# Weight pieces on GpSimd behind z's normalising, small products ahead of the weighted values, in an attention and feed-forward kernel

## The chip, the cores and the metric

One core of one Trainium2 chip runs the whole program. The metric is the device time of one execution in microseconds; of the kernel before there are three timed runs (291.29, 291.32 and 292.5; median 291.32) and one profiled execution. Lower is better.

## The reference

Eight batches of 256 tokens with 128 features go through one transformer block. In short:

```python
def _L0_attn_ref(x, W_qkv, b_qkv, W_out, b_out, rel_bias):      # 16 heads of 8
    qkv = (x @ W_qkv + b_qkv).reshape(B, S, 3, NHEAD, D_K)
    q, k, v = (qkv[:, :, 0], qkv[:, :, 1], qkv[:, :, 2])
    scores = jnp.einsum('bihd,bjhd->bhij', q, k) / jnp.sqrt(jnp.float32(D_K))
    scores = scores + bias_by_distance        # rel_bias, clipped at 128
    attn = jax.nn.softmax(scores, axis=-1)
    out = jnp.einsum('bhij,bjhd->bihd', attn, v).reshape(B, S, D)
    return out @ W_out + b_out
def _L0_ffn_ref(x, ...):                      # ternary weights, hidden 512
    h = jax.nn.silu(_tlin(x, w1_w, w1_s)) * _tlin(x, w2_w, w2_s)
    h = jax.nn.gelu(_tlin(h, h1_w, h1_s), approximate=False)
    h = jax.nn.gelu(_tlin(h, h2_w, h2_s), approximate=False)
    return _tlin(h, w3_w, w3_s)
x = x + _layernorm(_L0_attn_ref(_layernorm(x), ...))
x = x + _layernorm(_L0_ffn_ref(_layernorm(x), ...))
```

Everything is float32. The kernel keeps the precision by splitting operands into a high part (rounded to fp32r) and the rest, the low part.

## The kernel before

The five engines run programs of their own that are written out in order; semaphores tie them together. Nothing reorders at run time: an instruction that waits holds all that stands behind it on its engine. So the order of the work is the order of the code, and a change of order on one engine can make another wait.

The program has four parts.

**Start.** x comes in units of 2, 2, 4, 4 and 4 tiles of 128 tokens. For each unit VectorE takes moments (`x_moments`), GpSimd raises the variance to the power -0.5 (`x_inv_std`, L517; this text calls it the root), VectorE normalises (`x_normalize`, L620), TensorE transposes (`x_T`), ScalarE copies the result out (`keep_xT`), and TensorE multiplies with the weights of q, k and v. For batch 0 the rows of q and k are made by products of their own with spread-out weights (`row_products`), of which ScalarE takes the high part (`take`) and TensorE then subtracts it (`row_lows`). Beside this GpSimd casts the table of the position bias to fp32r, one slot pair of heads at a time (`table_high`, L525).

**Attention, steps b = 0 to 7.** A step has 8 slots s, one pair of heads each. In slot s TensorE computes `scores(b, s)` (L1270), then for the next batch `max_scores(b + 1, s)` (L1236) and `max_bias(b + 1, s)` (L1244), from which VectorE takes the row maxima (L685). ScalarE or VectorE writes the bias into the tile of a coming slot (`write_bias`, L1015 and L692), ScalarE takes the exponential (`probabilities`, L1008). The three tiles `place0` to `place2` go round: the maximum products of a slot may start when the exponential of the slot before is done, since they use its tile. After every second slot the values of two slot pairs are weighted (`weighted(b, g)`, L1296, group g of 4), and ScalarE copies the group out (`keep_weighted`, L1020). Between these stand the small products of the batch before: `back` (L1307, transposes of oT), `heads_T`, `project` (L1320), `maxima_T` (L1253, the transposed maxima, which ScalarE copies in `minus_max`), `norm_T` (L1327, transposes of z). The layer norms behind the projection run on VectorE in slots 4 to 6: `attn_moments`, `residual`, `second_norm`, the last of which normalises z (L620) and sets `z_set`.

**Splitting of the weights.** Eleven pieces of the feed-forward weights are split into high and low part by GpSimd (`split_weights`, L559 to L571, four instructions each, all reading the on-chip memory), in steps 1 to 6: 1, 1, 2, 3, 3 and 1 of them. In a step they stand behind the two roots that GpSimd computes for the layer norms.

**Feed-forward.** Four chunks of 512 tokens; `gate`, `layer1`, `layer2`, `layer3` on TensorE (L1441, L1442), in an order written out in `ffn`. The last batch's attention output (`heads_T`, `project`, the two norms, `norm_T`) is threaded through it.

## Time and profile before

| | us |
|---|---|
| median of three runs | 291.32 |
| the profiled execution | 292.18 |
| its span in the trace | 290.4 |
| TensorE busy | 268.5 (92%) |
| VectorE busy | 219.3 (76%) |
| ScalarE busy | 205.9 (71%) |
| GpSimd busy | 102.4 (35%) |
| start, to 31 us: TensorE busy | 28.88 |
| steps 1 to 6, 54 to 178 us: TensorE busy | 117.45 of 124.00 |
| the same: VectorE busy | 108.94 |
| the same: ScalarE busy | 91.22 |
| feed-forward, from 194 us: TensorE busy | 86.37 of 96.40 |
| ScalarE idle ahead of oT's copies (L1020), waiting for the weighted values | 22.1, 18 times |

The profiled execution is 1.8 us longer than its span: that is what lies around the recorded work. Busy times are sums over an engine; what a change is worth is not read from them but from the waits in the stretch where it acts. A row of a timeline gives start, length, engine, line, operation, output and input, the count of merged instructions, and in brackets how long the engine stood idle before it and what ended that. PE is TensorE (PEld its loading of weights), DVE VectorE, ACT ScalarE, POOL GpSimd. TensorE's clock was granted whole through the attention part (1.00, which is the 2.4 GHz level).

### The profile page before, as it was taken

The numbers are of one execution on the slowest core, as the hardware profiler recorded it, in microseconds if no ns is written. First come the engines' busy times: TensorE is split into PE (matmuls) and PEld (weight loads), VectorE is DVE, ScalarE is ACT, GpSimd is POOL, SyncE is SP. The second block draws the span as 40 slices with busy tenths as digits, with TensorE's granted clock in tenths as the row PEclk, the third lists the DMA queues.
The fourth block names the chain that finished last, engine by engine and source line by source line (L and its number), as shares of the span: only waits on it lengthen the run. The fifth ranks groups of instructions, "written<-read, shape, count | busy, mean of one in ns | idle before, by whom it ended". The sixth has DMA issues, their size and how long they took to land.

```text
span 290.4 us, 5171 instructions
## 1 busy us (share of the span) xinstructions
PE 268.5 (92%) x1875; PEld 180.4 (62%) x1875; DVE 219.3 (76%) x442; ACT 205.9 (71%) x316; POOL 102.4 (35%) x107
## 2 busy tenths in 40 slices
PE   7999989899999999999998998899999999999980
PEld 7756645555555554565554554567887888888860
DVE  3489977889789889889889899848556843673674
ACT  2777777776786786885886876777469976896750
POOL 7616000103504305906966957018630202400111
PEclk9999999999999999999999999999999999999996
DMA  6979506232221263470320200000000000010012
GB/s 166 320 238 142 184 11 208 89 83 77 74 76 38 77 207 124 138 224 8 104 81 19 61 1 3 1 3 1 0 2 0 0 0 2 0 36 2 2 36 77
DMA packets 21356, 21.17 MB, mean 73 GB/s; under 512 B 3664, under 2 KB 18768, under 8 KB 21072
## 3 DMA queue, kind: packets, MB, share of 16 engines
q1 hardware_dynamic: 20464, 20.53, 24.8%
q8 instruction: 17, 0.28, 0.4%
q10 hardware_dynamic: 864, 0.27, 0.4%
q14 instruction: 11, 0.09, 0.1%
HBM read 14.90 MB, written 5.64 MB: 71 GB/s over the span
## 4 chain that ended last, share of the span: by engine, by line
PE 60%; DVE 22%; ACT 9%; issue 5%; DMA 1%; POOL 0%; SPq 0%; ACTq 0%; DVEq 0%
PE place L1441 10%; PE place L1442 10%; PE place L1244 8%; DVE mx L685 7%; PE pv L1296 6%; PE place L1236 4%; ACT ring L1008 4%; DVE y_and_z L620 4%; PE place L1270 4%; DVE stats L609 2%; PE place L1195 2%; DVE place L692 2%; ACT place L1015 2%; PE pv L1442 2%; PE pv L1441 2%
## 5 line engine op out<-in xcount | busy, mean ns | idle before, releaser
L685 DVE TENSOR_REDUCE mx<-place 128x4 f32<-128x1024 f32 x64 | 78.1, 1222 | 13.1 <-PE place L1244 11.8
L517 POOL TENSOR_TENSOR rstd<-mv,mhalf 128x2 f32<-128x2 f32 (+1 forms) x26 | 21.0, 809 | 153.0 <-DVE mv L617 153.0
L1008 ACT ACTIVATE ring<-place 128x1024 f32<-128x1024 f32 x64 | 65.6, 1027 | 6.3 <-PE place L1281 3.0
L1244 PE MATMUL place<-room,identr 128*128 128x512 f32 x128 | 46.9, 447 | 0.0
L1015 ACT COPY place<-raw 128x1024 f32<-128x1024 f32 x37 | 37.7, 1022 | 12.2 <-DVE mx L685 11.9
L1441 PE MATMUL place<-room,w_hi 128*128 128x512 f32 (+1 forms) x116 | 44.6, 387 | 0.7 <-DVE room L818 0.7
L1442 PE MATMUL place<-room,w_hi 128*128 128x512 f32 (+1 forms) x116 | 44.0, 382 | 0.0
L818 DVE TENSOR_TENSOR room<-ring,room 128x512 fp32r<-128x512 f32 x32 | 21.4, 690 | 18.5 <-ACT room L1096 18.5
L1296 PE MATMUL pv<-ring,vx 128*9 128x256 f32 x512 | 33.6, 380 | 0.0
L1270 PE MATMUL place<-room 33*128 33x256 f32 x256 | 31.7, 328 | 1.1 <-DVE place L692 1.0
L1236 PE MATMUL place<-room 33*128 33x256 f32 x256 | 28.3, 297 | 2.9 <-ACT ring L1008 2.7
L1270 PEld LDWEIGHTS place<-room 33*128 33x128 f32 x256 | 18.9, 184 | 15.4 <-issue 12.2
L1020 ACT COPY oT<-pv 128x256 f32<-128x256 f32 x32 | 11.8, 370 | 22.2 <-PE pv L1296 22.1
L1236 PEld LDWEIGHTS place<-room 33*128 33x128 f32 x256 | 19.8, 185 | 10.1 <-issue 6.8
L1441 PEld LDWEIGHTS place<-room,w_hi 128*128 128x128 f32 x116 | 21.8, 188 | 5.1 <-DVE room L818 0.9
L1244 PEld LDWEIGHTS place<-room,identr 128*128 128x128 f32 x128 | 19.0, 188 | 8.6
L1442 PEld LDWEIGHTS place<-room,w_hi 128*128 128x128 f32 x116 | 21.8, 188 | 4.1
L692 DVE COPY place<-raw 128x1024 f32<-128x1024 f32 x19 | 23.2, 1225 | 0.6
L1094 ACT ACTIVATE ring<-place,hs 128x512 f32<-128x512 f32 x27 | 18.5, 686 | 5.9 <-PE place L1442 5.9
L1296 PEld LDWEIGHTS pv<-ring,vx 128*9 128x9 f32 x512 | 10.9, 90 | 17.3 <-issue 9.9
L830 DVE SCALAR_TENSOR_TENSOR ring<-place,hs,raw 128x512 f32<-128x512 f32 x16 | 12.0, 750 | 12.0 <-ACT raw L1073 11.8
L1096 ACT CAST room<-ring 128x512 fp32r<-128x512 f32 x32 | 19.9, 621 | 1.0
(141 smaller groups left out, 442.9 us busy)
## 6 DMA issues: line engine op xcount, KB each, us to landing
raw<-ext SPq DMA_DIRECT2D x8, 384.0 KB, 6.9
room<-q_parts SPq DMA_DIRECT2D x48, 64.0 KB
room<-k_parts SPq DMA_DIRECT2D x48, 64.0 KB
w_lo<-h SPq DMA_DIRECT2D x2, 1024.0 KB, 5.2
q_parts<-w_hi SPq DMA_DIRECT2D x4, 256.0 KB, 3.0
k_parts<-w_hi SPq DMA_DIRECT2D x2, 512.0 KB, 3.4
xs<-x SPq DMA_DIRECT2D x3, 256.0 KB, 5.7
w_lo<-w SPq DMA_DIRECT2D x3, 256.0 KB, 2.7
```

What stands on the lines that cost most here:

```text
L517: nc.gpsimd.tensor_tensor(rstd[:, at:at + width], mv[:, at:at + width, 1], mhalf[:, 0:width], ALU.pow).then_inc(rstd_set, 1)
L685: nc.vector.tensor_reduce(mx[:, s // RPAIRS, :, :, s % RPAIRS].rearrange("p i k -> p k i"), max_tile(b * PAIRS + s)[:, :, :].rearrange("p ...
L692: nc.vector.tensor_copy(score_tile(i)[:, :, :].rearrange("p k (j n) -> p k j n", j=2), pair_windows(raw[:, :, :], i % PAIRS)).then_inc(bia ...
L818: nc.vector.tensor_tensor(lo, act_f[:, half[c], k, :], hi.bitcast(F32), ALU.subtract).then_inc((a1_lo_set, a2_lo_set)[i], 1)
L1008: nc.scalar.activation(probs[:, s % PRING, :, :, :].rearrange("p k j n -> p (k j n)"), score_tile(b * PAIRS + s)[:, :, :].rearrange("p k n ...
L1015: nc.scalar.copy(score_tile(i)[:, :, :].rearrange("p k (j n) -> p k j n", j=2), pair_windows(raw[:, :, :], i % PAIRS)).then_inc(bias_set, 1)
L1236: mm(max_tile(b * PAIRS + s)[:, half, it * S:(it + 1) * S], rows(q_rows, b, half, s)[:, it * P:(it + 1) * P], rows(k_rows, b, half, s), st ...
L1244: last = mm(max_tile(b * PAIRS + s)[:, half, :], identr[:, :], windows(table_hi[:, 2 * s + half, :], 0, P, 2, S), start=False, stop=True, ...
L1270: last = mm(tile[:, half, j * S:(j + 1) * S], rows(k_rows, b, half, s)[:, j * P:(j + 1) * P], rows(q_rows, b, half, s), start=(s in BY_PE ...
L1296: last = mm(pv[32 * r:32 * r + VC, 0:S], vx[:, b * TPB + j, 4 * g + r, :], probs[:, (2 * g + r // 2) % PRING, r % 2, j, :], start=(j == 0) ...
L1441: mm(o, w, hi, start=first, stop=False)
L1442: done = mm(o, w, lo, start=False, stop=last and exact)
```

## The change

Six edits, all of order:

- GpSimd, start: the table's casts of slots 0 and 1 come ahead of the root of x's unit 2, and those of slots 6 and 7 wait until unit 3 is normalised (`xn_set` at 4).
- GpSimd, steps 1 to 6: the pieces of weights wait until z of the step is normalised (`z_set` at b).
- VectorE, start: moments of unit 1 behind the first normalising and the spread weights; `minus_ident` ahead of the second normalising.
- TensorE, start: both `row_products` and `row_lows(0)` ahead of the transposes of unit 1.
- TensorE, steps 0 to 6, slots 0, 2, 4 and 6: the weighted values come at the slot's end, behind the small products. In step 7 they stay. ScalarE copies group 3 behind the transposed maxima in steps 1 to 6.
- Feed-forward: the last `project` stands behind three outputs of layer 1 of chunk 1 and not two, and VectorE's last `attn_moments` behind one low part of that layer.

```diff
@@ -530,11 +530,16 @@
             pool.wait_ge(row_zeros, 1)
             spread_weights(nc.gpsimd.tensor_copy, 1)
             x_inv_std(1)
+            table_high(0)
+            table_high(1)
             x_inv_std(2)
-            for s in range(PAIRS):
+            for s in range(2, 6):
                 table_high(s)
-                if s == 5:
-                    x_inv_std(3)
+            x_inv_std(3)
+
+            pool.wait_ge(xn_set, 4)
+            table_high(6)
+            table_high(7)
             for i, s in enumerate(BY_PE):
                 pool.wait_ge(table_hi_pool, s + 1)
                 nc.gpsimd.tensor_tensor(table_lo[:, 2 * i:2 * i + 2, :], raw[:, 2 * s:2 * s + 2, :],
@@ -575,6 +580,8 @@
                 if b > 0:
                     inv_std((b - 1) * 2 + NU + 1, TPB)
                     inv_std((b - 1) * 2 + NU + 2, TPB)
+
+                    pool.wait_ge(z_set, b)
                 for piece in SPLIT_AT[b]:
                     split_weights(piece)
 
@@ -658,11 +665,11 @@
             x_moments(0)
             dve.wait_ge(qk_w_in[0], 16)
             nc.vector.tensor_scalar(wq_sb[:, :], wq_sb[:, :], scale, None, ALU.mult).then_inc(bq_scaled, 1)
-            x_moments(1)
             x_normalize(0)
             dve.wait_ge(row_zeros, 1)
             dve.wait_ge(bq_scaled, 1)
             spread_weights(nc.vector.tensor_copy, 0, (0,))
+            x_moments(1)
             dve.wait_ge(brows_in, 16)
             nc.vector.tensor_scalar(brows_sb[:, 0, 0:PAIRS], brows_sb[:, 0, 0:PAIRS], scale, None,
                                     ALU.mult).then_inc(brows_scaled, 1)
@@ -670,9 +677,9 @@
             nc.vector.tensor_tensor(low_bias[:, :, :], brows_sb[:, :, 0:PAIRS],
                                     brows_sb[:, :, PAIRS:PAIRS + 1].broadcast_to((P, 2, PAIRS)),
                                     ALU.mult).then_inc(low_bias_set, 1)
-            x_normalize(1)
             dve.wait_ge(ident_loaded, 16)
             nc.vector.tensor_scalar(minus_ident[:, :], ident[:, :], -1.0, None, ALU.mult).then_inc(minus_set, 1)
+            x_normalize(1)
             dve.wait_ge(qk_w_in[2], 16)
             nc.vector.tensor_scalar(bq_sb[:, 0:1], bq_sb[:, 0:1], scale, None, ALU.mult).then_inc(bq_scaled, 1)
             nc.vector.tensor_copy(identr[:, :], ident[:, :]).then_inc(identr_set, 1)
@@ -859,8 +866,9 @@
             gate_product(2, 3)
             gate_low(2, 3)
             layer_low(0, 0)
+            layer_low(1, 0, (0,))
             attn_moments(B - 1)
-            layer_low(1, 0, (0, 1))
+            layer_low(1, 0, (1,))
             residual(B - 1)
             layer_low(1, 0, (2, 3))
             second_norm(B - 1)
@@ -1036,9 +1044,11 @@
                         write_bias(ahead)
                     probabilities(b, s)
                     if s == 0:
-                        if b > 0:
+                        if b + 1 == B:
                             keep_weighted(b - 1, GROUPS - 1)
                         minus_max(b, 1)
+                        if 0 < b < B - 1:
+                            keep_weighted(b - 1, GROUPS - 1)
                     if b == 0:
                         if s == 1:
                             keep_xT(3)
@@ -1204,10 +1214,10 @@
 
             pe.wait_ge(xT_set, 1)
             row_products(0)
+            row_products(1)
+            pe.wait_ge(minus_set, 1)
+            row_lows(0)
             x_T(1)
-            pe.wait_ge(minus_set, 1)
-            row_products(1)
-            row_lows(0)
             pe.wait_ge(xT_set, 2)
             q_and_k(1, 0)
             q_and_k(1, 1)
@@ -1326,6 +1336,13 @@
                 for it in range(TPB):
                     last = nc.tensor.transpose(misc[:, it * P:(it + 1) * P], z[:, it, :], ident[:, :])
                 last.then_inc(zT_ready, 1)
+
+            def values(b, s):
+
+                if s > 0:
+                    weighted(b, s // 2 - 1)
+                elif b > 0:
+                    weighted(b - 1, GROUPS - 1)
 
             pe.wait_ge(identr_set, 1)
             for s in range(PAIRS):
@@ -1375,17 +1392,14 @@
 
                         scores(b, s + 1)
                         score_bias(b, s + 1)
+                    if s % 2 == 0 and not more:
+                        values(b, s)
                     if s == 0:
-                        if b > 0:
-                            weighted(b - 1, GROUPS - 1)
                         if b > 1:
                             pe.wait_ge(z_lo_set, b - 1)
                         if b == 0:
                             pe.wait_ge(qk_lo_set, 4)
                         maxima_T(b, 1)
-                    else:
-                        if s % 2 == 0:
-                            weighted(b, s // 2 - 1)
                     if b > 0:
                         if s == 1:
                             pe.wait_ge(mrow_set, b * RANGES + 2)
@@ -1432,6 +1446,8 @@
                         else:
                             pe.wait_ge(mrow_set, b * RANGES + 3)
                         norm_T(b - 1)
+                    if s % 2 == 0 and more:
+                        values(b, s)
             weighted(B - 1, GROUPS - 1)
 
             def product(o, weight, x, exact, first=True, last=True):
@@ -1560,9 +1576,9 @@
                 gate(2, 3, exact)
                 heads_T(B - 1)
                 layer1(0, 3, exact)
-                whole(layer1, 1, exact, (0, 1))
+                whole(layer1, 1, exact, (0, 1, 2))
                 project(B - 1)
-                whole(layer1, 1, exact, (2, 3))
+                layer1(1, 3, exact)
                 whole(layer2, 0, exact)
                 layer2(1, 0, exact)
                 pe.wait_ge(y_read, B)
```

On TensorE, in slots 2 to 4 of a middle step, the rows before are these (pv is the weighted values, misc<-ident,oT is `back`, misc<-ident,on `heads_T`, misc<-wo_sb,onT `project`, the place rows are scores, maximum products and maximum bias):

```order
L1236 MATMUL place<-room 128x256 x4
L1244 MATMUL place<-room,identr 128x512 x2
L1296 MATMUL pv<-ring,vx 9x256 x8
L1307 MATMUL misc<-ident,oT 128x128 x4
L1270 MATMUL place<-room 128x256 x4
L1236 MATMUL place<-room 128x256 x4
L1244 MATMUL place<-room,identr 128x512 x2
L1314 MATMUL misc<-ident,on 128x128 x2
L1270 MATMUL place<-room 128x256 x4
L1236 MATMUL place<-room 128x256 x4
L1244 MATMUL place<-room,identr 128x512 x2
L1296 MATMUL pv<-ring,vx 9x256 x8
```

and in the changed kernel, ten lines further down in the file:

```order
L1246 MATMUL place<-room 128x256 x4
L1254 MATMUL place<-room,identr 128x512 x2
L1317 MATMUL misc<-ident,oT 128x128 x4
L1306 MATMUL pv<-ring,vx 9x256 x8
L1280 MATMUL place<-room 128x256 x4
L1246 MATMUL place<-room 128x256 x4
L1254 MATMUL place<-room,identr 128x512 x2
L1324 MATMUL misc<-ident,on 128x128 x2
L1280 MATMUL place<-room 128x256 x4
L1246 MATMUL place<-room 128x256 x4
L1254 MATMUL place<-room,identr 128x512 x2
L1330 MATMUL misc<-wo_sb,onT 128x128 x2
```

In slot 2 the second `back` and in slot 4 `project` now stand ahead of the eight products of the weighted values. Slot 3 is as it was.

On TensorE at the start (misc<-ident,xn are the transposes of x, place<-ring,w_lo the row products, minus_ident the low rows, wq_sb and wk_sb unit 1's q and k), before:

```order
L1169 MATMUL misc<-ident,xn 128x128 x2
L1162 MATMUL place<-blank 128x256 x3
L1195 MATMUL place<-ring,w_lo 128x256 x2
L1169 MATMUL misc<-ident,xn 128x128 x2
L1195 MATMUL place<-ring,w_lo 128x256 x2
L1202 MATMUL place<-z_parts,minus_ident 128x512
L1174 MATMUL place<-ring,wq_sb 128x256
L1174 MATMUL place<-ring,wk_sb 128x256
```

and now:

```order
L1179 MATMUL misc<-ident,xn 128x128 x2
L1172 MATMUL place<-blank 128x256 x3
L1205 MATMUL place<-ring,w_lo 128x256 x4
L1212 MATMUL place<-z_parts,minus_ident 128x512
L1179 MATMUL misc<-ident,xn 128x128 x2
L1184 MATMUL place<-ring,wq_sb 128x256
L1184 MATMUL place<-ring,wk_sb 128x256
```

The second transposes, of unit 1, moved behind the second row products and the first low rows; q and k of unit 1 follow right behind them.

On VectorE at the start (L609 and L616 are the moments, L620 and L627 the normalising), before:

```order
L660 TENSOR_SCALAR wq_sb<-wq_sb 128x128
L609 BN_STATS stats<-xs 128x6 x2
L613 BN_AGGR mv<-stats 128x2 x2
L617 TENSOR_SCALAR mv<-mv 128x2
L620 TENSOR_SCALAR xn<-xs,mv,rstd 128x128 x2
L382 COPY w_lo<-wq_sb 128x8x32
L667 TENSOR_SCALAR brows_sb<-brows_sb 128x8
L670 TENSOR_TENSOR low_bias<-brows_sb 128x16
L620 TENSOR_SCALAR xn<-xs,mv,rstd 128x128 x2
L675 TENSOR_SCALAR minus_ident<-ident 128x128
```

and now:

```order
L667 TENSOR_SCALAR wq_sb<-wq_sb 128x128
L627 TENSOR_SCALAR xn<-xs,mv,rstd 128x128 x2
L382 COPY w_lo<-wq_sb 128x8x32
L616 BN_STATS stats<-xs 128x6 x2
L620 BN_AGGR mv<-stats 128x2 x2
L624 TENSOR_SCALAR mv<-mv 128x2
L674 TENSOR_SCALAR brows_sb<-brows_sb 128x8
L677 TENSOR_TENSOR low_bias<-brows_sb 128x16
L681 TENSOR_SCALAR minus_ident<-ident 128x128
L627 TENSOR_SCALAR xn<-xs,mv,rstd 128x128 x2
```

The first normalising and the spread weights moved ahead of the second moments, which stand ahead of the bias rows; `minus_ident` moved ahead of the second normalising.

## Rows read from the trace of the kernel before

**Rows 1.** The chain of waits of step 5: start us, length us, what
```profile
138.03 0.51 PE place L1236 x4
...
145.00 0.36 ACT oT L1020
...
147.38 0.50 PE place L1236 x4
...
148.55 0.98 PE pv L1296 x16
...
149.53 0.66 PE misc L1320 x4
```

**Rows 2.** Timeline of VectorE, normalising (columns as above under the table)
```profile
23.73 3.75 DVE L620 TENSOR_SCALAR xn<-xs,mv,rstd 128x128 f32<-128x128 f32 x4
...
53.45 1.12 DVE L620 TENSOR_SCALAR xn<-xs,mv,rstd 128x128 f32<-128x128 f32 x4
...
155.78 1.74 DVE L620 TENSOR_SCALAR y_and_z<-xs,mv,rstd 128x128 f32<-128x128 f32 x2
```

**Rows 3.** Timeline of TensorE, step 5
```profile
143.53 1.05 PE L1296 MATMUL pv<-ring,vx 128*9 128x256 f32 x16
...
152.22 0.30 PEld L1236 LDWEIGHTS place<-room 33*128 33x128 f32 x4 [0.28 <-ACT ring L1008]
...
155.53 1.09 PE L1281 MATMUL place<-room,identr 128*128 128x512 f32 x4
...
157.68 0.41 PE L1327 MATMUL misc<-ident,y_and_z 128*128 128x128 f32 x2 [1.06 <-DVE y_and_z L620]
...
158.36 0.40 PE L1236 MATMUL place<-room 33*128 33x256 f32 x4
```

**Rows 4.** Timeline of ScalarE and TensorE, end of step 2
```profile
94.68 1.03 ACT L1008 ACTIVATE ring<-place 128x1024 f32<-128x1024 f32 x1 [0.34 <-PE place L1281]
...
94.99 0.44 PE L1327 MATMUL misc<-ident,y_and_z 128*128 128x128 f32 x2 [0.35 <-DVE w_hi L640]
...
95.85 0.50 PE L1236 MATMUL place<-room 33*128 33x256 f32 x4
```

**Rows 5.** Timeline of GpSimd, end of step 5's pieces and the next root
```profile
168.89 1.27 POOL L571 TENSOR_TENSOR xn<-xn,w_hi 128x512 f32<-128x512 f32 x1
...
171.93 0.73 POOL L517 TENSOR_TENSOR rstd<-mv,mhalf 128x2 f32<-128x2 f32 x1 [1.77 <-DVE mv L617]
```

**Rows 6.** Timeline of ScalarE, slots 4 and 5 of step 5
```profile
149.60 0.37 ACT L1020 COPY oT<-pv 128x256 f32<-128x256 f32 x1 [1.17 <-PE pv L1296]
...
150.19 1.02 ACT L1015 COPY place<-raw 128x1024 f32<-128x1024 f32 x1 [0.23 <-DVE mx L685]
```

**Rows 7.** Timeline of step 0, slots 3 to 6
```profile
44.42 0.74 DVE L640 SCALAR_TENSOR_TENSOR w_hi<-misc,bq_sb,w_hi 128x512 fp32r<-128x512 f32 x1
...
45.63 1.16 PE L1180 MATMUL misc<-wv_sb,xT 128*128 128x128 f32 x8
...
45.76 0.37 ACT L1020 COPY oT<-pv 128x256 f32<-128x256 f32 x1 [0.87 <-PE pv L1296]
...
48.60 0.40 PE L1236 MATMUL place<-room 33*128 33x256 f32 x4
```

**Rows 8.** Timeline of the start
```profile
5.21 1.20 POOL L382 COPY w_lo<-wk_sb 128x256 f32<-128x256 f32 x2
...
6.57 0.60 DVE L620 TENSOR_SCALAR xn<-xs,mv,rstd 128x128 f32<-128x128 f32 x2
...
10.35 0.37 ACT L940 COPY ring<-misc 128x256 f32<-128x256 f32 x1
...
10.84 0.63 PE L1174 MATMUL place<-ring,wq_sb 128*128 128x256 f32 x2
```

**Rows 9.** Timeline of TensorE, the last projection
```profile
220.12 0.71 PE L1320 MATMUL misc<-wo_sb,onT 128*128 128x128 f32 x4 [0.69 <-ACT onT L1024]
```

## The prediction

> **What bounds the kernel now.** I read the chain of waits of one middle step of the attention loop first, then the timelines of TensorE, ScalarE and VectorE through that step, and at last those of the start, the first step and the place of the last projection. Steps are called 0 to 7 (one batch each), slots are the eight head pairs of a step. All times below are in step 5, which TensorE's maximum products open at 138.03, unless said.
>
> TensorE is the busiest engine, but it runs in a ring with ScalarE: the maximum products of a slot go into the tile that the exponential of the slot before has left. The chain [rows 1] shows what this means: at 145.00 ScalarE copies the first group of weighted values out (oT), then writes a bias, then does an exponential, and only at 147.38 TensorE goes on with slot 4's maximum products. Behind these the path runs through the weighted values (0.98) and the projection (0.66), and at the step's end through z's normalising on VectorE. The reader is to see that two things of the change lie on this chain, z and the order of values and projection, and that a third lies on it too: the copy oT, which is fed by the very product that the change puts back.
>
> **GpSimd's pieces behind z's normalising.** z's two instructions take 1.74 beside GpSimd's pieces; four such instructions without company take 1.12 at 53.45, so two take 0.56, and about 1.2 us per step leave VectorE. At 23.73 four take 3.75, beside GpSimd's casts of the bias table [rows 2]. How much of that reaches TensorE? In step 5 it waits 1.06 for z, but its maximum products of the next step, at 158.36, also wait for slot 7's exponential, which waits for the score bias that ends at 155.53 plus 1.09, 156.62 [rows 3]. In step 2 that second wait is seen bare: the exponential starts at 94.68, z's transposes come late by 0.35, and the maximum products start at 95.85, 1.17 after the exponential's start [rows 4]. So in steps 2 to 4 the faster z gives nothing; in step 5 the products could start at 158.0, 0.35 earlier, and step 6 is alike. Gain 0.8 at the highest, and only if the ring is not later by then.
>
> The Trainium skill (SBUF — State Buffer, Who interferes with whom) says that VectorE's copies and tensor_scalar in their 2-port modes take the port pair that GpSimd uses, whoever comes first holding it for a whole instruction. The 3.75 against 1.12 agrees. By that rule the change also makes new collisions at the start; they are priced from rows below.
>
> The last instruction of step 5's pieces now begins at 168.89 and takes about 1.3; the next root is asked for at 171.93 [rows 5]. That is 1.8 of room, against pieces that start later by z's own time and one hand-over, about 1.2. It fits; if not, the root is late by a few tenths, and VectorE behind it has 1.2 in hand from z.
>
> **Small products ahead of the weighted values, steps 1 to 6.** TensorE's total is the same, but ScalarE runs in order, and its copy of a group waits for the weighted values. Slot 2: group 0's values start at 143.53 and the transposes behind them take about 0.6 [rows 3]. Exchanged, with 0.15 of wait for VectorE's `on` ahead, the values end at about 145.33 and the copy starts at 145.40, not at 145.00. This copy is on the chain, so slot 4's maximum products are 0.40 later. Slot 4: the values ended at 149.53 [rows 1]; with the 0.40 and the projection's 0.66 ahead they end at 150.59. The copy, which waited 1.17 for them already, starts at 150.66 and not at 149.60. The bias of slot 6 behind it, which started at 150.19 because VectorE's maximum held it [rows 6], now waits for the copy. In [rows 1] the maximum products start 2.38 behind the copy's start; from 150.66 that is 153.04, against 152.22 [rows 3]: +0.82. The hand-over at slot 6 is shorter (2.03 from the bias's start, and 0.26 for the copy ahead of it), which gives 152.95, +0.73. I take 0.75. From there TensorE has no idle time to the step's end, so steps 1 to 4 lose it whole: 3.0. In steps 5 and 6 the wait for z covers most: the score bias ends at 157.37, the exponential starts at 157.41, the maximum products at 158.58 against 158.36. That is 0.2 each, 0.4, and holds z's gain already.
>
> What comes back? The projection is earlier for VectorE, but VectorE is at its maximum of slot 4 until just before 150.19, as ScalarE's wait for it shows [rows 6], and the projection ended at 150.19 as well [rows 1]: the add of y starts there either way. Bounds of this part: nothing if all is absorbed, 0.82 for each of four steps at the top.
>
> **Step 0.** Here q's product goes ahead of group 0 and v's ahead of group 1. v must wait for k's low part, which VectorE finishes at 44.42 plus 0.74, 45.16. TensorE would be there at about 44.3 (the values began 0.98 ahead of v's 45.63, and q's lead gives 0.3 to 0.4), and idles where the values stood. v runs from 45.2 to 46.3, the values to 47.3, the copy starts at 47.4 (was 45.76), and the maximum products 2.3 to 2.4 later, at 49.75 against 48.60 [rows 7]: +1.15. At the least 0, if k's low part came a whole us earlier, which q's lead is too small for.
>
> **The start.** x's first normalising no longer stands behind the second load. Its root is there when GpSimd goes on at 5.21, so it may start at 5.3 and not at 6.57; but GpSimd copies weights until 6.41, and by the slow instructions of [rows 2] it gets through about 0.4 earlier, not 1.2. Against that the transposes of unit 1 now stand behind the low rows, which wait for ScalarE's taking. Before, ScalarE's xT copy stood right behind that taking, at 10.35, and q's product of unit 1 at 10.84 [rows 8]. Now low rows 0.4, transposes 0.4, and two hand-overs of 0.07 come in between: +0.95. Less 0.4 that is 0.55, and two casts of the table beside x's second normalising may add to it; bounds -0.4 (the collision costs nothing and the order nothing) and +1.0; I take 0.6. The later normalising at 23.73 frees VectorE 2.6 earlier, but TensorE's row products set the pace there: 0.
>
> **The feed-forward part.** The last projection waits 0.69 for onT [rows 9]; behind one more output of layer 1 it doesn't, and the engine is full behind it: -0.6 (bounds -0.7 and 0). VectorE's last moments move behind one more low part; z's transposes come only after five outputs of layer 2, which covers it.
>
> **Sum.** 0.6 + 1.15 + 3.0 + 0.4 - 0.6 = +4.5. The profiled execution took 292.18 (span 290.4 and 1.8 around it), which gives 296.7. It is 0.86 above the median of 291.32, so for the median the forecast is 295.8.
>
> **Rivals.**
> Faster: VectorE's chain is the true bound, and the ring with ScalarE has slack that the rows don't show. For it speaks that the chain of waits walks through values, projection and z. Then the waits at z go: 1.06 and as much in step 6, 0.35 and as much in two more, 3.1 in all; with start and feed-forward even, this is 288.2. Against it: ScalarE's copy is on the same chain, and in step 2 the maximum products start with the exponential whatever z does.
> No change: the values' delay is swallowed, and start, z and projection cancel: 0.6 - 0.8 - 0.6, plus something in step 0, about 291. What decides is whether slot 6's maximum products stay at 14.2 us behind the step's first (152.22 less 138.03).
> Worse: the later pieces reach the next root in steps 4 and 5, which have three each, and cost a us there on top: 298.
>
> **Chances.** Forecast 0.62, faster 0.18, no change 0.15, worse 0.05. What a measurement can tell here is about 0.5%, 1.5 us. From the cases: faster 0.19, same 0.18, slower 0.63. The slower case's own range is 293.4 to 297.6 (0.4 to 0.82 for each step, the start at -0.1 to 1.0, step 0 from 0.6). For 8 in 10 it reaches down to 289.8, which leaves out most of the faster rival and the worse one.
>
> **What would show it.** z's two instructions at 0.6 in steps 2 to 6. ScalarE's copy of group 1 waiting 1.9 or more for TensorE where it waited 1.17. TensorE's maximum products in a middle step 0.4 later at slot 4 and 0.75 at slot 6, counted from the step's first. The three steps from 95.85 to 158.36 take 62.5 now, 20.8 each; I expect 64.2. A TensorE gap of 0.9 ahead of v in step 0. q of unit 1 at 11.4. No wait at the last projection. I am wrong if those three steps take 62.5 or less, or if q of unit 1 starts before 10.84.

## The result and the profile after

The changed kernel takes 293.22 us (median of six, 292.96 to 294.12) against 291.87 for the kernel before beside it: ratio 1.0052 [1.0037, 1.0068], slower by 1.5 us. The forecast was 295.8, slower by 4.5. Ratios, and the differences in us that are worked out from them, leave out the few runs that fell in a slower state, while medians and ranges hold them, so that the two can differ by some tenths. The profiled execution took 293.34 (before 292.18), with a span of 291.4 (before 290.4).

The first place to look was the distance between the openings of the steps (the maximum products of slot 0 on TensorE; in step 7, which has none, the weighted values in their place, at 178.66 and 181.53), since a loss in the loop must stand there:

| stretch | before | after | change | forecast |
|---|---|---|---|---|
| q of unit 1 starts | 10.84 | 11.44 | +0.60 | +0.60 |
| from there to step 1's opening (54.12; 55.75) | 43.28 | 44.31 | +1.03 | +1.15 |
| step 1 | 20.65 | 20.99 | +0.34 | +0.75 |
| step 2 | 21.08 | 21.47 | +0.39 | +0.75 |
| step 3 | 21.07 | 21.46 | +0.39 | +0.75 |
| step 4 | 21.11 | 21.48 | +0.37 | +0.75 |
| step 5 | 20.33 | 20.21 | -0.12 | +0.20 |
| step 6 | 20.30 | 20.17 | -0.13 | +0.20 |
| step 7 and on to the last transposes of heads | 34.91 | 34.94 | +0.03 | 0 |
| from there to z's last transposes, in the feed-forward part | 19.83 | 18.87 | -0.96 | -0.60 |

They add up to +1.94, and VectorE's last instruction ends 1.95 later too (288.90 against 286.95). The span is only 1.0 longer, because the output's transfer behind that instruction took 2.5 us in this trace and 3.45 in that of before. So a single pair of traces is good to a microsecond at its end, and the distances between openings to some hundredths.

TensorE in step 5 of the changed kernel, start and length, with the idle time before and what ended it; this answers to [rows 1, 3]:

```profile
141.15 0.50 PE L1246 MATMUL place<-room 33*128 33x256 f32 x4 [0.55 <-ACT ring L1016]
...
146.66 0.66 PE L1317 MATMUL misc<-ident,oT 128*128 128x128 f32 x4
147.25 1.05 PE L1306 MATMUL pv<-ring,vx 128*9 128x256 f32 x16
...
150.76 0.50 PE L1246 MATMUL place<-room 33*128 33x256 f32 x4 [0.45 <-ACT ring L1016]
151.19 0.73 PE L1254 MATMUL place<-room,identr 128*128 128x512 f32 x2
151.77 0.61 PE L1330 MATMUL misc<-wo_sb,onT 128*128 128x128 f32 x4
152.30 1.05 PE L1306 MATMUL pv<-ring,vx 128*9 128x256 f32 x16
...
155.72 0.51 PE L1246 MATMUL place<-room 33*128 33x256 f32 x4 [0.39 <-ACT ring L1016]
...
159.05 1.10 PE L1291 MATMUL place<-room,identr 128*128 128x512 f32 x4
159.99 0.38 PE L1337 MATMUL misc<-ident,y_and_z 128*128 128x128 f32 x2
...
161.36 0.50 PE L1246 MATMUL place<-room 33*128 33x256 f32 x4 [0.56 <-ACT ring L1016]
```

z's transposes wait for nothing now, and the opening behind them waits 0.56 for the exponential instead. Slot 4 waits 0.45 (it was 0.22) and slot 6 waits 0.39; before, the products of slot 6 showed no wait, but the load of their weights waited 0.28 [rows 3]. ScalarE beside it, answering to [rows 6]:

```profile
148.37 0.37 ACT L1028 COPY oT<-pv 128x256 f32<-128x256 f32 x1 [0.24 <-PE pv L1306]
...
153.42 0.37 ACT L1028 COPY oT<-pv 128x256 f32<-128x256 f32 x1 [1.62 <-PE pv L1306]
153.69 1.02 ACT L1023 COPY place<-raw 128x1024 f32<-128x1024 f32 x1
154.64 1.03 ACT L1016 ACTIVATE ring<-place 128x1024 f32<-128x1024 f32 x1
```

The copy at 153.42 waits 1.62 where it waited 1.17, and bias and exponential follow it without a break. In the chain of waits (start, length, what) the path goes through just these:

```profile
152.37 1.03 PE pv L1306 x16
153.40 0.02 issue
153.42 0.03 ACT oT L1028
153.45 0.24 issue
153.69 0.16 ACT place L1023
153.85 0.79 issue
154.64 1.04 ACT ring L1016
155.68 0.04 issue
155.72 0.51 PE place L1246 x4
```

Over the whole kernel, TensorE's idle time ahead of the maximum products rises from 2.9 to 7.4 (columns: busy, mean ns | idle before, releaser). The 4.5 more is not all loss: z's waits, which are gone, were 3.1 together, and TensorE is 1.4 us less busy in all (267.1 against 268.5).

```profile
L1246 PE MATMUL place<-room 33*128 33x256 f32 x256 | 28.5, 299 | 7.4 <-ACT ring L1016 7.4
L1028 ACT COPY oT<-pv 128x256 f32<-128x256 f32 x32 | 11.9, 373 | 29.4 <-PE pv L1306 29.3
```

VectorE and GpSimd. z's two instructions in step 5, then the normalising at the start and that of unit 3, answering to [rows 2, 8]:

```profile
5.32 1.20 DVE L627 TENSOR_SCALAR xn<-xs,mv,rstd 128x128 f32<-128x128 f32 x2 [0.76 <-POOL rstd L517]
...
8.51 1.08 DVE L627 TENSOR_SCALAR xn<-xs,mv,rstd 128x128 f32<-128x128 f32 x2 [0.38 <-POOL rstd L517]
...
24.38 1.11 DVE L627 TENSOR_SCALAR xn<-xs,mv,rstd 128x128 f32<-128x128 f32 x4
...
158.96 0.60 DVE L627 TENSOR_SCALAR y_and_z<-xs,mv,rstd 128x128 f32<-128x128 f32 x2
```

1.74 has become 0.60 and 3.75 has become 1.11, while the first two, which moved beside GpSimd's work, take twice what they took. GpSimd's pieces start behind z, and the root behind step 5's pieces still finds the engine free, as those behind steps 1 to 4 do (with 1.48 us and more to spare), answering to [rows 5]:

```profile
174.90 0.72 POOL L517 TENSOR_TENSOR rstd<-mv,mhalf 128x2 f32<-128x2 f32 x1 [0.62 <-DVE mv L624]
```

Start, step 0 and the last projection, answering to [rows 7 to 9]:

```profile
11.44 0.70 PE L1184 MATMUL place<-ring,wq_sb 128*128 128x256 f32 x2 [0.46 <-ACT ring L948]
...
45.63 1.16 PE L1190 MATMUL misc<-wv_sb,xT 128*128 128x128 f32 x8 [0.77 <-DVE w_hi L647]
...
223.97 0.61 PE L1330 MATMUL misc<-wo_sb,onT 128*128 128x128 f32 x4
```

### The profile page after: what moved, and what is told of

Its sections match the earlier page's. It is cut to its first block, busy times and chain, and to the rows that moved or that the text cites. A ratio compares the mean times of both kernels' runs of the same rounds, so it can differ in the third digit from the quotient of the medians.

```text
span 291.4 us, 5174 instructions
## 1 busy us (share of the span) xinstructions
PE 267.1 (92%) x1875; PEld 182.9 (63%) x1875; DVE 212.1 (73%) x442; ACT 204.8 (70%) x316; POOL 102.5 (35%) x107
## 3 DMA queue, kind: packets, MB, share of 16 engines
HBM read 14.90 MB, written 5.64 MB: 70 GB/s over the span
## 4 chain that ended last, share of the span: by engine, by line
PE 76%; ACT 10%; DVE 7%; issue 5%; POOL 0%; DVEq 0%; ACTq 0%
PE place L1254 11%; PE place L1457 11%; PE place L1458 10%; PE pv L1306 10%; PE place L1246 6%; ACT ring L1016 6%; PE place L1280 4%; PE misc L1317 3%; PE place L1291 3%; ACT place L1023 2%; PE place L1205 2%; PE place L1172 2%; DVE place L699 2%; PE pv L1458 2%; PE pv L1457 2%
## 5 line engine op out<-in xcount | busy, mean ns | idle before, releaser
L692 DVE TENSOR_REDUCE mx<-place 128x4 f32<-128x1024 f32 x64 | 78.3, 1224 | 22.4 <-PE place L1254 21.1
```

The lines of the kernel that those rows point to most:

```text
L692: nc.vector.tensor_reduce(mx[:, s // RPAIRS, :, :, s % RPAIRS].rearrange("p i k -> p k i"), max_tile(b * PAIRS + s)[:, :, :].rearrange("p ...
```

## Experiments

Two theories went in. The ring: ScalarE's copies of weighted values wait for the later values and hold the exponentials that TensorE waits for. The rival: VectorE's chain through projection and z bounds the steps. Each kernel is compared with the kernel before on the same chip.

**The changed kernel with the values' order undone** on TensorE and ScalarE (start, z and feed-forward edits stay); of the edit, the core of TensorE's part:

```diff
-                    if s % 2 == 0 and more:
-                        values(b, s)
+                    else:
+                        if s % 2 == 0:
+                            weighted(b, s // 2 - 1)
```

> The changed kernel with the order of the weighted values undone, on TensorE and on ScalarE; z's wait, start and feed-forward part stay. Ring theory (ScalarE's copy of a group waits for the values, and the copy holds the exponential that TensorE waits for): step 0 gives back 1.0 and steps 1 to 4 0.38 each, steps 5 and 6 come out at 0.35 to 0.45 below before; the kernel is 2.5 to 3 faster than the changed one, 1.0 to 1.3 below before. VectorE theory (VectorE's chain bounds the steps, values ahead of the projection are on it): undoing costs time, it comes out slower than the changed kernel by 1 or more.

Measured 290.91, ratio 0.9969 [0.9954, 0.9984], so 0.9 below before and 2.4 below the changed kernel. Steps 2 to 4 take 21.09, 21.10 and 21.14, step 5 takes 19.97. The values' order makes the whole loss and more, though its undoing brought a little less than the 2.5 to 3 expected.

**The values' order alone**, put into the kernel before (TensorE's order and ScalarE's copy of group 3, nothing else); of the edit:

```diff
+                    if s % 2 == 0 and more:
+                        values(b, s)
```

> The kernel before with only the order of the values changed (TensorE, and ScalarE's copy of group 3). Ring theory: step 0 +1.0, steps 1 to 4 +0.38 each, steps 5 and 6 +0.2 each with z still late: +2.9 in all, and TensorE's maximum products in slot 6 stand 0.38 later behind the step's first. VectorE theory: -1 or better in steps 1 to 6 and +1.0 in step 0, so about 0 or below.

Measured 295.09 (median of six), ratio 1.0108 [1.0083, 1.0132]: +3.15 (2.4 to 3.9), where undoing it brought 2.4. The waits at slots 4 and 6 are those of the changed kernel. In addition z, still slow here, is waited for:

```profile
150.54 0.50 PE L1238 MATMUL place<-room 33*128 33x256 f32 x4 [0.44 <-ACT ring L1008]
...
155.49 0.50 PE L1238 MATMUL place<-room 33*128 33x256 f32 x4 [0.39 <-ACT ring L1008]
...
160.63 0.41 PE L1329 MATMUL misc<-ident,y_and_z 128*128 128x128 f32 x2 [0.71 <-DVE y_and_z L620]
```

From slot 7's maximum products to the next opening it is 3.41 in step 2 (94.56 to 97.97) against 3.20 in the changed kernel (95.01 to 98.21). But slot 0 behind the late opening is 0.1 shorter (2.53 in steps 3 and 4, against 2.64). So steps 2, 3 and 4 take 21.67, 21.56 and 21.52 where the changed kernel takes 21.47, 21.46 and 21.48: where the values stand late, the faster z is worth 0.20, 0.10 and 0.04. The next run shows what it is worth where they stand early.

**GpSimd's wait for z alone**:

```diff
+                    pool.wait_ge(z_set, b)
                 for piece in SPLIT_AT[b]:
```

> The kernel before with only GpSimd's wait for z ahead of the pieces of weights. Ring theory: z's two instructions fall to 0.6, steps 2 to 4 stay as long as they were (bound by slot 7's exponential), steps 5 and 6 lose 0.35 to 0.45 each: -0.8. VectorE theory: TensorE's waits for z of 1.06, 1.05 and three times 0.3 all go, -3. If it is 0, the pieces that come later cost elsewhere what they give.

Measured 291.51, ratio 0.9989 [0.9976, 1.0002]. Steps 2 to 4 take 21.09, 21.10 and 21.12, as before; steps 5 and 6 19.97 and 19.99, so 0.36 and 0.31 less than before. TensorE at the end of steps 4 and 5:

```profile
137.54 0.38 PE L1329 MATMUL misc<-ident,y_and_z 128*128 128x128 f32 x2
...
138.91 0.50 PE L1238 MATMUL place<-room 33*128 33x256 f32 x4 [0.56 <-ACT ring L1010]
...
158.88 0.50 PE L1238 MATMUL place<-room 33*128 33x256 f32 x4 [0.45 <-ACT ring L1010]
```

z's wait is gone and 0.56 for the exponential stands there. The rival wanted 3 us and falls, as far as z is concerned. In time the gain is 0.3, with an interval that just reaches no change.

**The start's edits alone** (GpSimd, VectorE, TensorE) and **the feed-forward edit alone**, of the latter TensorE's part:

```diff
-                whole(layer1, 1, exact, (0, 1))
+                whole(layer1, 1, exact, (0, 1, 2))
                 project(B - 1)
-                whole(layer1, 1, exact, (2, 3))
+                layer1(1, 3, exact)
```

> The kernel before with only the edits of the start (GpSimd's casts, VectorE's moments, TensorE's row products and low rows ahead of unit 1's transposes). Ring theory, and the trace of the changed kernel: q of unit 1 at 11.4 and not 10.84, and this 0.6 stays to the end: +0.6. If the start's shift is swallowed by a later wait (TensorE waits 0.66 for VectorE's bias in step 0): 0.

> The kernel before with only the feed-forward edits (the last projection behind three outputs of layer 1, and VectorE's last moments one low part later). The forecast's term was -0.6, the trace of the changed kernel shows 0.96 less between the last transposes of the heads and those of z: -0.7 to -1.0. If the wait only moves (layer 2 waits instead, or z's transposes do): 0.

The start: 292.26, ratio 1.0023 [1.0010, 1.0037], +0.7 (0.3 to 1.1). Its one trace, of the shortest of its twelve runs, does not show where: q of unit 1 starts at 11.01, near the 10.84 of before, and VectorE's last instruction ends 0.24 later than before. The feed-forward edit: 290.57, ratio 0.9959 [0.9943, 0.9974], -1.2. The projection's wait of 0.69 [rows 9] is gone in its trace. That is more than the wait; a part of the rest is that this projection costs 0.61 and not 0.71.

**z, the last normalising of x and the feed-forward edit together**, the start's other edits and the values as before; the line that no kernel above has:

```diff
+                if s == 6:
+                    pool.wait_ge(xn_set, 4)
                 table_high(s)
```

> The kernel before with GpSimd's wait for z, its wait for x's third normalising ahead of the table's slots 6 and 7, and the feed-forward edits; neither the values' order nor the other edits of the start. Sum of the parts: -0.3 to -0.8 for z, -0.7 to -1.0 for the projection, 0 for x's normalising: -1.0 to -1.8, the fastest so far. If the parts don't add, it is not below the values-undone kernel by the start's 0.6.

Measured 290.41, ratio 0.9945 [0.9927, 0.9964], -1.6. The parts that help do so without the two that don't.

**The projection alone ahead of the values** (slot 4 of steps 1 to 6, in the kernel before):

```diff
-                    if s % 2 == 0 and not more:
+                    if s % 2 == 0 and not (more and s == 4 and b > 0):
                         values(b, s)
...
+                    if s % 2 == 0 and (more and s == 4 and b > 0):
+                        values(b, s)
```

> The kernel before with only the projection ahead of the values of slot 4, in steps 1 to 6. Forecast's arithmetic: the copy of group 1 comes 0.66 later, of which 0.33 show at slot 6: +0.33 in steps 1 to 4. By the trace of the changed kernel, where the projection holds the values by 0.44: +0.12 each, 0.5 in all, with steps 5 and 6 at nothing. If the chain of waits were the bound (values ahead of the projection on it): -0.98 per step.

Measured 292.73, ratio 1.0032 [1.0017, 1.0048], +0.9. TensorE in slot 4 and at slot 6:

```profile
148.17 0.50 PE L1236 MATMUL place<-room 33*128 33x256 f32 x4 [0.23 <-ACT ring L1008]
148.60 0.73 PE L1244 MATMUL place<-room,identr 128*128 128x512 f32 x2
149.18 0.61 PE L1320 MATMUL misc<-wo_sb,onT 128*128 128x128 f32 x4
149.71 1.05 PE L1296 MATMUL pv<-ring,vx 128*9 128x256 f32 x16
150.69 0.50 PE L1270 MATMUL place<-room 33*128 33x256 f32 x4
...
153.13 0.50 PE L1236 MATMUL place<-room 33*128 33x256 f32 x4 [0.39 <-ACT ring L1008]
```

The projection puts the values 0.53 behind itself (149.18 to 149.71), not 0.66, and it starts 0.58 behind the maximum bias where the values started 0.67 behind it (147.81 and 148.48 in the trace of before). So the values are late by 0.44. The scores behind both come 2.52 after the slot's opening and not 2.72: the same instructions take 0.2 less in this order. From slot 4's opening to slot 6's it is 6.24, 6.25 and 6.27 in steps 2 to 4, where before has 6.13, 6.13 and 6.17: the order of slot 4 alone costs the ring 0.11, as was expected. Less of it is left at the end of the step, since slot 0 is 0.1 shorter in steps 3 and 4 (2.63 against 2.73): in steps 2 to 4 slot 7's maximum products stand 17.99, 17.90 and 17.92 behind the opening, against 17.89, 17.88 and 17.92. A further 0.2 to 0.3 a step are lost at z, whose transposes wait 0.70 to 0.80 where they waited 0.26 to 0.35: from slot 7 to the next opening it is 3.49, 3.47 and 3.39 against 3.19 each. So steps 2 to 4 take 21.48, 21.37 and 21.31, that is 0.40, 0.30 and 0.20 more than before. In steps 5 and 6, where z was late anyway, the early projection helps it: z's waits fall from 1.06 and 1.05 to 0.77 and 0.80, and these steps take 0.26 and 0.14 less. From step 0's opening to step 7's this kernel takes 0.60 more than before.

**The changed kernel with ScalarE's copies later**: group 0 behind slot 3's exponential and group 1 behind slot 5's, so that no bias and no exponential stands behind a waiting copy. If the ring theory holds, the loss must go although TensorE's order stays.

```diff
-                    if s >= 2 and s % 2 == 0:
-                        keep_weighted(b, s // 2 - 1)
+                    if b + 1 == B or b == 0:
+                        if s >= 2 and s % 2 == 0:
+                            keep_weighted(b, s // 2 - 1)
+                    elif s in (3, 5, 6):
+                        keep_weighted(b, (s - 2) // 2)
```

> The changed kernel, and in steps 1 to 6 ScalarE copies group 0 behind slot 3's exponential (not slot 2's) and group 1 behind slot 5's exponential and the transposed maxima (not slot 4's). Nothing is left out. Ring theory: the copies no longer hold the exponentials, TensorE's waits at slots 4 and 6 fall from 0.45 and 0.39, steps 1 to 4 lose the 0.38 that they gained and more, since the values behind the projection cost TensorE itself 0.2 less: -1.5 to -3 against the changed kernel. Rival (the order on TensorE itself costs, for instance the products of the next slot behind the values): no gain, or slower, as the values wait for the late copy.

Measured 293.13, ratio 1.0056 [1.0025, 1.0086], with twelve runs from 291.39 to 295.52. Its trace was of one of the short ones (291.81), with steps 2 to 4 of 21.10, 21.10 and 21.12: the ring's loss gone, the median not. So the same instructions ran once more:

> The same instructions as the changed kernel with late copies, for another trace of it: its timed runs lay between 291.4 and 295.5, its trace at 289.9. If this trace is long (292 or more), the stretch where it is longer names what spreads; if it is short again, that stays open. Ring theory expects steps 1 to 4 at 21.1 in either.

Measured 291.38 (eight runs, 291.02 to 291.60), ratio 0.9972 [0.9951, 0.9993]. Here the loss is gone in time too: 0.8 below before, where the changed kernel stands 1.5 above it, with the same order on TensorE. Its step 5 on TensorE, and ScalarE's two copies:

```profile
139.29 0.50 PE L1249 MATMUL place<-room 33*128 33x256 f32 x4 [0.55 <-ACT ring L1016]
...
148.25 0.50 PE L1249 MATMUL place<-room 33*128 33x256 f32 x4
...
153.46 0.50 PE L1249 MATMUL place<-room 33*128 33x256 f32 x4 [0.45 <-ACT ring L1016]
```

```profile
148.28 0.38 ACT L1028 COPY oT<-pv 128x256 f32<-128x256 f32 x1
...
151.43 1.02 ACT L1023 COPY place<-raw 128x1024 f32<-128x1024 f32 x1 [1.85 <-DVE mx L692]
...
153.55 0.36 ACT L1028 COPY oT<-pv 128x256 f32<-128x256 f32 x1
```

Neither copy waits, slot 4 isn't waited for at all and opens 8.96 behind the step's first (148.25; it was 9.35), and slot 6's bias waits 1.85 for VectorE's maximum. This is the bound that the kernel before has too: there slot 6's bias starts 12.16 behind the opening (150.19 less 138.03), released by the same maximum, and here 12.14 (151.43 less 139.29). The chain of waits of this kernel shows where the path went:

```profile
147.79 1.24 DVE mx L692
149.02 0.02 issue
149.05 1.23 DVE place L699
150.28 1.12 DVE mx L692
```

**The same two ideas without the start's edits**: late copies with the values in their new order from step 1 on, and late copies with the values in their old order (edits as above, combined).

> The faster parts together: GpSimd's wait for z and for x's third normalising, the feed-forward edits, the values behind the small products from step 1 on (not in step 0), and ScalarE's copies of groups 0 and 1 behind the exponentials of slots 3 and 5 in steps 1 to 6; the start as before. Ring theory: steps 2 to 4 as short as before or shorter (21.1), steps 5 and 6 at 19.8, projection -0.9: 289.6 to 290.2, a little below the kernel with z's wait and feed-forward edits (290.4). Rival (the late copies bring something of their own that the trace of the first such run doesn't show, since its times spread from 291.4 to 295.5): times that spread again, the median at 291 or above.

> As the kernel with z's wait, x's third normalising and the feed-forward edits, values in the old order, with ScalarE's late copies of groups 0 and 1 in steps 1 to 6. Ring theory: TensorE's wait of 0.22 at slot 4 goes, up to 0.2 per step, 1 in all: 289.5 to 290.4. If the late copies alone make the times spread, they spread here too and the order of the values has no part in it.

With the new order: 293.17, from 289.92 to 294.75, ratio 1.0012 [0.9975, 1.0048]; its trace, again of a short run, has a span of 288.0. With the old order: 290.29, from 289.61 to 290.85, ratio 0.9925 [0.9899, 0.9952]. This is the fastest kernel of the study, 0.75% under before and so faster than both, though its interval overlaps that of z, x's normalising and the feed-forward edit together (0.9945). In its trace steps 2 to 4 take 21.11, 21.06 and 21.13, and with the new order they take 21.10, 21.07 and 21.13: once the copies stand late, the order on TensorE costs these steps nothing. The late copies bring them nothing either: with the old order slot 4 no longer waits and opens at 9.06 in step 5, where it was 9.35, but the 0.2 a step that was hoped for does not come.

The old order with late copies does not spread (seven runs within 1.3 us), so late copies alone don't make a kernel spread. The new order with late copies has runs up to 5 us apart in two measurements of three; of these two, one is of instructions that did not spread in the third, on another chip, and the other was taken on that chip. The mean granted clock of each run tells more: in both measurements the long runs have the lower clocks. Of the first measurement (the changed kernel with late copies) the runs from 291.39 to 292.49 have 0.988 to 0.993, those from 293.10 to 293.86 have 0.982 to 0.986, and the three of 295 us have 0.971 to 0.975. Of the other (without the start's edits) the runs from 289.92 to 291.14 have 0.990 to 0.992, the two up to 292.45 have 0.985 and 0.986, and those from 293.89 on 0.970 to 0.976. The runs of before on these two chips lie at 0.987 to 0.994, but for one of 294.28 at 0.983. So the spread goes with the clock. Where in the kernel the clock was lower, why in these kernels, and whether the steps were longer in such a run, stays open: no long run was traced.

## Why the prediction was wrong

**The sign, the mechanism and two of the five terms held.** From q of unit 1 to step 1's opening it is 1.03 more for 1.15, 0.97 of it in step 0 itself, with v waiting 0.77 for k's low part where 0.9 was forecast. The start cost 0.7 in time for 0.6. That q of unit 1 came 0.60 later in this pair of traces is luck: over five traces with the start of before it stands at 10.73 to 11.70, over the five with the changed start at 11.01 to 11.44, so this mark cannot show the term. z came down to 0.60, and in the run of z alone that gave nothing in steps 2 to 4 and 0.36 in step 5, where 0 and 0.35 were worked out. GpSimd's pieces ended 0.62 before the next root was asked for.

**The term that failed is "steps 1 to 4 lose 0.75 each", 3.0 in all.** They lost 0.34 to 0.39 each, 1.49. The chain of it was right: copy of group 1, bias of slot 6, exponential, TensorE, and from there nothing regained to the step's end. Only the last link differs in steps 1 to 4, the ones that lose. There ScalarE copies the transposed maxima (mrow) behind the exponential, and ahead of slot 6 TensorE has work on a later unit of x (its transposes, q, k or v), which waits for this copy. Step 3, first before and then changed:

```profile
107.99 1.02 ACT L1015 COPY place<-raw 128x1024 f32<-128x1024 f32 x1 [0.22 <-DVE mx L685]
...
110.26 1.13 PE L1174 MATMUL misc<-xT,wk_sb 128*128 128x512 f32 x2 [0.30 <-ACT mrow L993]
```

```profile
110.73 1.02 ACT L1023 COPY place<-raw 128x1024 f32<-128x1024 f32 x1
...
112.99 1.13 PE L1184 MATMUL misc<-xT,wk_sb 128*128 128x512 f32 x2 [0.62 <-ACT mrow L1001]
```

VectorE's maximum of slot 4 ends 12.11 us behind the opening before and 12.13 in the changed kernel (107.96 less 95.85, 110.34 less 98.21). The bias of slot 6 starts at 12.14 before (107.99) and at 12.52 in the changed kernel (110.73), held by the copy. This 0.38 is what the step loses.

The size of the term's input was wrong. The prediction had the copy of group 1 late by 1.06 (149.60 to 150.66), made of two numbers:

- "Slot 4's maximum products are 0.40 later": measured 0.26 (9.61 behind the opening against 9.35). The sum put the transposes' 0.6 ahead of the values, and 0.15 of wait for `on` ahead of that, both counted from where the values had stood. The values do start 0.59 behind the transposes. But the transposes start 5.51 behind the opening (146.66 less 141.15), just where the values had stood (143.53 less 138.03, 5.50 [rows 3]). The wait is there: VectorE's `on` ends at 146.61, and the transposes start 0.77 behind the maximum bias, where those of slot 1, which wait for nothing, start 0.57 behind it. It costs nothing, because TensorE would have been there 0.2 earlier than the sum took: slot 2 opens 0.10 earlier (4.41 behind the step's opening against 4.51), and transposes follow a maximum bias by 0.57 where values follow it by 0.66.
- "The projection's 0.66 ahead": measured 0.44, from starts, in the changed kernel (151.19 to 152.30 is 1.11, against 0.67 from maximum bias to values before) and in the run of the projection alone. 0.66 is what the chain gives the projection between values and scores [rows 1]. A duration that belonged to an order was taken as if it belonged to the instruction.

So the copy is late by 0.70 (12.27 behind the opening, against 11.57), and the mark "waiting 1.9 or more" read 1.62. From the copy to the maximum products it is 2.30 now (153.42 to 155.72), and the prediction's shorter hand-over of 2.03 and 0.26 gave 2.29; before it was 2.62, since the bias waited for VectorE's maximum and not for the copy alone. This fixed 0.32 is absorbed first. An error of a third in the copy (0.70 for 1.06) therefore became one of a half in the step (0.38 for 0.73). The three steps from step 3's opening to step 6's took 63.15, where 64.2 was expected.

**Steps 5 and 6** went down by 0.12 and 0.13 where +0.2 each was forecast, from the same input: slot 6 is 0.38 late and the next opening follows 5.64 behind it (155.72 to 161.36), which the prediction had as 5.61.

**The feed-forward part** brought 0.96 in the trace and 1.2 in time, for 0.6. A tenth is the projection between other neighbours (0.61 for 0.71); the rest was not taken apart. The forecast had counted only its wait of 0.69.

With 1.49 for 3.0, -0.25 for 0.4 and -0.96 for -0.6 the sum of 4.5 falls to the 1.94 of the trace. In time, the parts measured alone (+3.15, -0.3, -1.2, +0.7) add to 2.35 for the 1.5 of the whole; their intervals leave room for that. In the traces the loop does add up. From step 0's opening to step 7's the values' order alone brings +2.82 and z alone -0.64, together 2.18, and the changed kernel shows 2.21.

The recorded sums hold two slips, which don't carry the miss: the five terms give 4.55, and the slower case's own range, from the bounds stated beside it, comes out at 293.2 to 296.6 and not at 293.4 to 297.6. The measured 293.22 lies at its foot.

**The rivals.** That the waits for z bound the steps is refuted by z alone. That VectorE's maxima do is not refuted: with late copies in the new order slot 4 opens 0.4 earlier, steps 2 to 4 still take 21.07 to 21.13, and the chain holds two maxima and a bias of VectorE in a row. The same maximum releases slot 6's bias in the kernel before. So the rival was wrong in its wait and its price, while a part of VectorE's chain seems to set the 21.1 of these steps, before as well. No run made that chain shorter, so this is read from the waits and not tested. The row of no change was to be decided by slot 6 at 14.2, and it stands at 14.57. The later pieces reached no root.

The Trainium skill (SBUF — State Buffer, Who interferes with whom) has VectorE's 2-port modes and GpSimd take the shared ports in turn, a whole instruction at a time. The traces agree both ways: 3.75 became 1.11 when GpSimd's casts were moved away, and 0.60 [rows 8] became 1.20 at 5.32, where the change put two normalisings beside two of GpSimd's copies of 1.20 in all.

## What to carry to other kernels

In a kernel whose engines wait on each other like these, a copy that empties an accumulator belongs where nothing urgent stands behind it on its engine: which of two products comes first on TensorE matters less than what the copy's wait holds up. Removing one wait is worth only what the next one leaves, and the quick z had three values here as the other wait moved: nothing in steps 2 to 4 of the kernel before, 0.04 to 0.20 in the same steps with the values late, and 0.31 to 0.36 in steps 5 and 6 of the kernel before. When small instructions change neighbours, take from the trace the distance between starts in a like sequence, not the duration in the old one, and lay the moved sequence over the old start by start before adding any wait to it.

## What was not expected of the hardware

- The same three groups of slot 4 (maximum bias, values, projection) occupy TensorE for 2.29 us in the old order (147.81 to 150.10) and for 2.09 with the projection ahead (148.60 to 150.69 in the run of the projection alone); at slot 0, with the transposed maxima as the small product, it is 1.96 in the old order (138.47 to 140.43) and 1.86 in the new (141.59 to 143.45, changed kernel). So the small products ahead give TensorE 0.1 to 0.2 a slot. Why was not tested.
- Steps 2 to 4 of the six kernels with the old order and early copies all take 21.07 to 21.14. But q of unit 1 started at 10.84 and at 11.70 in two kernels with the same start (before, and z alone), although from there to step 0's opening it is 22.48 and 22.47, and the time behind VectorE's last instruction differed by 0.95 between two traces. Openings of steps can be compared to hundredths; the start and the end of a single trace can't.
